# First unit in two sets of four, aggregation ahead of the last z2 store, and twelve last normalizations on VectorE in a GNN with LSTM windows

## The reference

```python
x = _layernorm(x + _L0_gnn_ref(...), axis=-1)      # x1
...
    agg = jnp.einsum('nm,bmd->bnd', A_hat, features)
    x = agg.reshape(-1, d)
    h = jax.nn.relu(_batchnorm(x @ W1.T + b1, g1, be1))
    out = h @ W2.T + b2
    out = _batchnorm(out, g2, be2)                 # over all graphs and nodes
...
x = _layernorm(x + _L1_gnn_ref(...), axis=-1)      # rows of 128 features
```

## Time and profile before

| | |
|---|---|
| median of 3 runs | 840.4 us (840.08 to 840.74) |
| the profiled execution's own time | 839.27 us |
| its span | 837.5 us |
| TensorE busy | 805.8 us, 96% |
| VectorE busy | 704.6 us, 84% |
| ScalarE busy | 593.3 us, 71% |
| GpSimd busy | 68.9 us, 8% |
| end of the last z2 store | 774.5 us |
| first scaling of the last stage | 777.2 us |
| last normalization ends | 835.0 us |

### The profile page before, as it was taken

How to read it: one execution, slowest core, us unless ns; L and a number is a source line. 1 busy time by engine, 2 the same in 40 slices (tenths; PEclk the granted TensorE clock), 3 DMA queues, 4 the chain that set the end, 5 groups by cost and what they waited for, 6 DMA issues and landing times.

```text
span 837.5 us, 15410 instructions
## 1 busy us (share of the span) xinstructions
PE 805.8 (96%) x4872; PEld 517.8 (62%) x4872; DVE 704.6 (84%) x1795; ACT 593.3 (71%) x1186; POOL 68.9 (8%) x58
## 2 busy tenths in 40 slices
PE   8999999999999999999999999999999977999984
PEld 7667677567757765776567657765675653333542
DVE  5678989888988898898889888998989986677995
ACT  4777777767776677767776777677776762990498
POOL 0000000000000000000000000000000001000674
PEclk9999999999999999999999999999999999999998
DMA  6000010201120012001100110011010110344244
GB/s 214 29 26 2 1 55 22 76 1 36 43 77 0 25 50 75 0 25 50 63 12 25 50 45 31 26 51 51 1 51 2 51 41 36 100 142 133 77 163 188
DMA packets 17691, 44.94 MB, mean 54 GB/s; under 512 B 2032, under 2 KB 3184, under 8 KB 17520
## 3 DMA queue, kind: packets, MB, share of 16 engines
q1 hardware_dynamic: 17648, 44.39, 14.9%
HBM read 27.61 MB, written 16.78 MB: 53 GB/s over the span
## 4 chain that ended last, share of the span: by engine, by line
PE 77%; issue 9%; DVE 9%; ACT 3%; SPq 1%; POOL 0%; DMA 0%; ACTq 0%; DVEq 0%; POOLq 0%
PE gate_bank L812 15%; PE gate_bank L813 15%; PE gate_bank L797 9%; PE gate_bank L828 6%; PE gate_bank L838 6%; PE back_bank L770 3%; PE front_bank L735 3%; PE front_bank L741 3%; PE front_bank L729 3%; PE front_bank L724 3%; DVE bn L1022 3%; PE gate_bank L821 3%; ACT z L940 2%; PE back_bank L778 1%; PE back_bank L780 1%
## 5 line engine op out<-in xcount | busy, mean ns | idle before, releaser
L812 PE MATMUL gate_bank<-h_hi,w_hi 128*128 128x256 f16 (+2 forms) x528 | 165.2, 313 | 5.1 <-DVE h_lo L1115 4.8
L813 PE MATMUL gate_bank<-h_hi,w_lo 128*128 128x256 f16 (+2 forms) x528 | 164.6, 312 | 0.0
L890 ACT ACTIVATE gate_i<-gate_bank,lstm_bias 128x256 f32<-128x256 f32 (+2 forms) x176 | 99.9, 572 | 71.1 <-PE gate_bank L838 58.7
L890 ACT ACTIVATE gate_o<-gate_bank,lstm_bias 128x512 f32<-128x512 f32 (+2 forms) x176 | 99.7, 571 | 35.5 <-PE gate_bank L838 21.1
L828 PE MATMUL gate_bank<-h_lo,w_hi 128*128 128x256 f16 (+2 forms) x384 | 117.7, 306 | 0.0
L1099 DVE SCALAR_TENSOR_TENSOR gate_f<-gate_o,gate_f 128x512 f32<-128x512 f32 (+2 forms) x176 | 95.1, 540 | 23.7 <-ACT gate_f L896 22.9
L812 PE MATMUL gate_bank<-s_hi,w_hi 128*128 128x256 f16 (+2 forms) x384 | 112.5, 301 | 0.5 <-DVE s_hi L1112 0.5
L813 PE MATMUL gate_bank<-s_hi,w_lo 128*128 128x256 f16 (+2 forms) x384 | 112.4, 301 | 0.0
L890 ACT ACTIVATE gate_g<-gate_bank,lstm_bias 128x256 f32<-128x256 f32 (+2 forms) x176 | 100.2, 569 | 6.3 <-PE gate_bank L838 3.3
L838 PE MATMUL gate_bank<-s_lo,w_hi 128*128 128x256 f16 (+2 forms) x384 | 102.4, 302 | 0.0
L896 ACT ACTIVATE gate_f<-cell 128x512 f32<-128x512 f32 (+2 forms) x176 | 88.8, 510 | 16.2 <-DVE cell L1090 9.8
(11 more groups left out here) (162 smaller groups left out, 1573.3 us busy)
## 6 DMA issues: line engine op xcount, KB each, us to landing
x_front<-in_x SPq DMA_DIRECT2D x16, 512.0 KB, 4.4
rows_sb<-in_x SPq DMA_DIRECT2D x16, 512.0 KB, 3.3
x_kept<-normed_sb SPq DMA_DIRECT2D x16, 512.0 KB, 2.7
z<-x_kept SPq DMA_DIRECT2D x16, 512.0 KB, 3.6
out<-z SPq DMA_DIRECT2D x15, 512.0 KB, 3.1
z<-in_wr SPq DMA_DIRECT2D x1, 1536.0 KB, 6.5
out<-z SPq DMA_DIRECT2D x2, 256.0 KB, 2.2
wih_sb<-in_wih SPq DMA_DIRECT2D x1, 192.0 KB, 2.4
```

The costliest lines, as they stand in the source:

```text
L812: mm(dst, w[0], v[0], start=start, stop=False)
L813: mm(dst, w[1], v[0], start=False, stop=False)
L890: ins = activation(acts[gate][h][:, 0:n], gate_bank[h][bank_of(job, gate)][:, 0:n], ACT.Tanh if gate == "g" else ACT.Sigmoid, bias=lstm_bi ...
```

## The change

Three edits in the stretch after the first part.

First, the z2 loop on VectorE runs one turn less and the last turn is written out. The last chunk's statistics signal by a semaphore of their own (`sem_bn2_all`), aggregation and the two small sums come right behind them, and the last chunk's store (`keep_z2`) stands behind the sums, ahead of the wait for GpSimd's power.

Second, the first unit is taken in two sets of four graphs (`first_terms`). VectorE makes two scalings (units 0 and 1), then statistics and moments of the first bank with the scaling of unit 2 behind step 1, then those of the second bank with the shift of the first four graphs behind step 0 and the scaling of unit 3 behind step 1, then the scaling of the first unit of pass 1. The shift of the other four stands in the next unit. GpSimd makes two powers of four columns for this unit, and ScalarE normalizes it in two parts. For this ScalarE's pass 0 is written out and its loop starts at 1. Semaphore counts of u = 0 are one signal (or four) higher from then on.

Third, in the last pass ScalarE normalizes units 0, 1 and four graphs of unit 2. VectorE normalizes the other four of unit 2 (`normed_here`, mean subtracted and rstd multiplied, so that no shift is needed) behind its last moments, then waits for the last power and normalizes the eight of unit 3. SyncE waits for `y_shared` and `y_norm[2]` before the store of unit 2; the last two stores wait for VectorE's `y_last`. The last shift is gone.

```diff
@@ semaphores, SyncE @@
+        sem_bn2_all = sem("bn2_moments_complete")
+        y_shared = sem("y_shared_normed")
...
-            for u in range(3):
+            for u in range(2):
                 store(HALVES // 4 - 1, u)
+            sp.wait_ge(y_shared, 1)
+            store(HALVES // 4 - 1, 2)
             for n in range(2):
                 sp.wait_ge(y_last, n + 1)
@@ GpSimd @@
             def row_powers(t, u):
-                pool.wait_ge(y_mom[u], 4 * t + 4)
+                if (t, u) == (0, 0):
+                    for n in range(2):
+                        at = slice(4 * n, 4 * n + 4)
+                        pool.wait_ge(y_mom[0], 4 * n + 4)
+                        nc.gpsimd.tensor_tensor(rstd[0][:, at], veps[0][:, at], neg_half[:, at], ALU.pow
+                                                ).then_inc(y_rstd[0], 1)
+                    return
+                pool.wait_ge(y_mom[u], 4 * t + 4 + 4 * (u == 0))
                 nc.gpsimd.tensor_tensor(rstd[u][:], veps[u][:], neg_half[:], ALU.pow).then_inc(y_rstd[u], 1)
@@ ScalarE @@
-            def normed_rows(t, u, last=False):
-                act.wait_ge(y_shift[u], t + 1)
-                for b in range(GB):
+            def normed_rows(t, u, graphs=range(GB)):
+                for b in graphs:
...
-                    if last and b == 3:
-                        ins.then_inc(y_last, 1)
-                ins.then_inc(y_last if last else y_norm[u], 1)
-
-            with act.Fori(0, HALVES // 4 - 1) as t:
+                return ins
+
+            def four_normed(t, first=False):
                 for u in range(4):
-                    normed_rows(t, u)
-            for u in range(4):
-                normed_rows(HALVES // 4 - 1, u, u == 3)
+                    if first and u == 0:
+                        for n in range(2):
+                            act.wait_ge(y_shift[0], n + 1)
+                            ins = normed_rows(0, 0, range(4 * n, 4 * n + 4))
+                    else:
+                        act.wait_ge(y_shift[u], t + 1 + (u == 0))
+                        ins = normed_rows(t, u)
+                    ins.then_inc(y_norm[u], 1)
+
+            four_normed(0, True)
+            with act.Fori(1, HALVES // 4 - 1) as t:
+                four_normed(t)
+            LAST = HALVES // 4 - 1
+            for u in range(2):
+                act.wait_ge(y_shift[u], LAST + 1 + (u == 0))
+                normed_rows(LAST, u).then_inc(y_norm[u], 1)
+            act.wait_ge(y_shift[2], LAST + 1)
+            normed_rows(LAST, 2, range(4)).then_inc(y_norm[2], 1)
@@ VectorE @@
+            with dve.Fori(0, CHUNKS // 2 - 1) as c:
                 for h in range(2):
...
+                    z2_stats(c, h)
+                    keep_z2(c, h)
+            z2_stats(CHUNKS // 2 - 1, 0)
+            keep_z2(CHUNKS // 2 - 1, 0)
+            z2_stats(CHUNKS // 2 - 1, 1).then_inc(sem_bn2_all, 1)
+            dve.wait_ge(sem_bn2_all, 1)
             ve.bn_aggr(mv[:, 0, :], z_moments[:, 0, :, :].rearrange("p c s -> p (c s)")).then_inc(sem_bn2, 1)
             dve.wait_ge(sem_bn2, 1)
             ve.tensor_tensor(small[:, 14:15], mv[:, 0, 0:1], v2_sb[:, 0:1], ALU.add)
             ve.tensor_scalar_add(small[:, 12:13], mv[:, 0, 1:2], EPS).then_inc(sem_bn2, 1)
+            keep_z2(CHUNKS // 2 - 1, 1)
             dve.wait_ge(sem_bn2_pow, 1)
...
+            def first_terms(n, between):
+
+                at = slice(4 * n, 4 * n + 4)
+                dve.wait_ge(y_full[0], n + 2)
+                row_stats(row_bank[0][n], bn[0], n).then_inc(y_mom[0], 1)
+                for step in range(3):
+                    dve.wait_ge(y_mom[0], 4 * n + step + 1)
+                    row_moments(bn[0][:, at, :], comb[0][:, :, at], veps[0][:, at], step).then_inc(y_mom[0], 1)
+                    between[step]()
...
+            def terms(t, u, scaled=True):
+                shift = (lambda: row_shift(t, u - 1) if u > 1 else row_shift(t + 1, 0)) if u else lambda: row_shift(t - 1, 3)
+                row_terms(t, u, (shift, (lambda: scale_z2(dve, 0, t + 1, u)) if scaled else nothing, nothing))
+
+            def normed_here(u, n):
+
+                for b in range(4 * n, 4 * n + 4):
+                    last = ve.tensor_scalar(z[:, CHUNKS - 8 + 2 * u + n, 1, (b % 4) * P:(b % 4 + 1) * P],
+                                            row_bank[u][n][:, (b % 4) * P:(b % 4 + 1) * P], comb[u][:, 2, b:b + 1],
+                                            rstd[u][:, b:b + 1], ALU.subtract, ALU.mult)
+                return last
+
+            dve.wait_ge(sem_bn2, 5)
+            for u in range(2):
+                scale_z2(dve, 0, 0, u)
+            first_terms(0, (nothing, lambda: scale_z2(dve, 0, 0, 2), nothing))
+            first_terms(1, (lambda: row_shift(0, 0, slice(0, 4)), lambda: scale_z2(dve, 0, 0, 3), nothing))
+            scale_z2(dve, 0, 1, 0)
+            row_terms(0, 1, (lambda: row_shift(1, 0, slice(4, 8)), lambda: scale_z2(dve, 0, 1, 1), nothing))
+            for u in range(2, 4):
+                terms(0, u)
+            LAST = HALVES // 4 - 1
+            with dve.Fori(1, LAST) as t:
                 for u in range(4):
-                    scale = nothing if last else lambda: scale_z2(dve, 0, t + 1, u)
...
+                    terms(t, u)
             for u in range(4):
-                scale_z2(dve, 0, 0, u)
-            LAST = HALVES // 4 - 1
-            four_rows(0, True, False)
-            with dve.Fori(1, LAST) as t:
-                four_rows(t, False, False)
-            four_rows(LAST, False, True)
-            row_shift(LAST, 3)
+                terms(LAST, u, False)
+            normed_here(2, 1).then_inc(y_shared, 1)
+            dve.wait_ge(y_rstd[3], LAST + 1)
+            for n in range(2):
+                normed_here(3, n).then_inc(y_last, 1)
```

More of the change, by code:

```diff
@@ L1037, in row_moments @@
                                                    op1=ALU.mult)
-                return ve.scalar_tensor_tensor(out=veps_t[:], in0=m2, scalar=1.0 / P, in1=apart, op0=ALU.mult,
+                return ve.scalar_tensor_tensor(out=veps_t, in0=m2, scalar=1.0 / P, in1=apart, op0=ALU.mult,
                                                op1=ALU.add)
@@ L1060, in back_rows @@
                     wait(dve, ("back", "moments", n - 1) if n else ("back", "stats", 1), g, h)
[L1061 removed]
+                    ins = row_moments(bn[0][:], comb[0][:], veps[0][:], n)
                 elif what == "normed":
@@ L1135, in _, with z2_stats, keep_z2 @@
             ve.tensor_tensor(small[:, 10:12], v1_sb[:, 2, :], small[:, 14:16], ALU.subtract).then_inc(sem_bn1, 1)
-            with dve.Fori(0, CHUNKS // 2) as c:
-                for h in range(2):
[L1140 to L1148, removed]
+            def z2_stats(c, h):
+                dve.wait_ge(z2_full[h], c + 1)
+                return ve.bn_stats(z_moments[:, 0, bass.ds(2 * c + h, 1), :].rearrange("p o s -> p (o s)"),
+                                   gate_bank[h][0][:])
+            def keep_z2(c, h):
+                ve.tensor_scalar(z[:, bass.ds(2 * c + h, 1), 0, :].rearrange("p o n -> p (o n)"),
+                                 gate_bank[h][0][:], v2_sb[:, 0:1], None, ALU.add).then_inc(z2_kept[h], 1)
+            with dve.Fori(0, CHUNKS // 2 - 1) as c:
+                for h in range(2):
+                    z2_stats(c, h)
[4 more added lines that the diff above has]
+            dve.wait_ge(sem_bn2_all, 1)
             ve.bn_aggr(mv[:, 0, :], z_moments[:, 0, :, :].rearrange("p c s -> p (c s)")).then_inc(sem_bn2, 1)
@@ L1177, in four_rows @@
-            def four_rows(t, first, last):
-                def nothing():
-                    pass
-                for u in range(4):
-                    scale = nothing if last else lambda: scale_z2(dve, 0, t + 1, u)
-                    if u:
-                        shift = lambda: row_shift(t, u - 1)
-                    else:
-                        shift = nothing if first else lambda: row_shift(t - 1, 3)
-                    row_terms(t, u, (shift, scale, nothing))
-            dve.wait_ge(sem_bn2, 5)
@@ new lines, in row_shift, with nothing @@
+            def row_shift(t, u, at=slice(0, GB)):
+                dve.wait_ge(y_rstd[u], t + 1)
+                ve.scalar_tensor_tensor(out=mean_rstd[u][:, at], in0=comb[u][:, 2, at], scalar=-1.0,
+                                        in1=rstd[u][:, at], op0=ALU.mult, op1=ALU.mult).then_inc(y_shift[u], 1)
+            def nothing():
+                pass
+            def terms(t, u, scaled=True):
+                shift = (lambda: row_shift(t, u - 1) if u > 1 else row_shift(t + 1, 0)) if u else lambda: row_shift(t - 1, 3)
+                row_terms(t, u, (shift, (lambda: scale_z2(dve, 0, t + 1, u)) if scaled else nothing, nothing))
```

7 lines of the change are left out of this document (2 added, 5 removed).

## The result

In seven runs each, the changed kernel has a median of 838.05 us (836.75 to 839.41), the kernel before 840.26 us (839.04 to 841.2). The ratio of the two is 0.9975 with a 95% interval of 0.9963 to 0.9987, so 2.1 us faster, between 1.1 and 3.1. A later set of runs of the same two kernels gave 838.71 against 839.71 us, 0.9990 (0.9978 to 1.0002), which alone could not tell the change from nothing. The forecast of 839.05 us said 1.35 us less.

A forecast was written before the change was run, and what follows sets the result against it. VectorE bounds the last stage until near 821 us, then ScalarE's backlog and the last stores. Tail -1.8 plus start offset +0.45 gives -1.35 us: from the median of 840.4 to 839.05 us, range 838.0 to 840.0.

The forecast's parts named there:

- Aggregation: VectorE after the last z2 statistics: aggregation ahead of the last z2 store starts 0.65 us earlier, the store covered.
- the second half: VectorE's second set of four in the first unit, with the first shift: 2.06 us.
- unit 1: VectorE's unit after the first, with the second shift: 2.86 us in place of 3.15, so -0.29.
- the hold by GpSimd: First unit: GpSimd's fourth scaling holds VectorE's small instructions up to 0.28 us; half taken, +0.14.
- the offset: VectorE's delay from the first units, carried through the steady part: +0.45 us, range 0 to +0.8.
- ScalarE's early start: ScalarE begins the first unit at about 782.5, not 784.9; worth nothing at the end.
- Tail: Last pass, twelve rows moved to VectorE: -1.8 us with the stores, -2.3 by arithmetic alone.
- Queue: Last stores at the kernel's end: their queue ends 0.5 us later than arithmetic alone.
- (b): Rival: the start keeps its gain (offset 0) or arithmetic binds the tail (-2.3): 838.4 us, chance 0.25.
- (a): The forecast: stores bind the tail and the start loses its gain: 839.05 us, 838.5 to 839.6, chance 0.56.
- (c): Rival in the tail: VectorE's normalization out of PSUM holds GpSimd's last power up to 1.2 us: 839.75, chance 0.12.
- (d): Rival: GpSimd's scaling falls on VectorE's in each steady unit, +5.3 us, total 844.4, chance 0.04.

The follow-up runs named there:

- the run with 12 fillers and the last reload apart: Changed kernel with 12 TensorE fillers, not 20, and the last x1 reload waited for ahead of the last pass alone: stretch 62.35 us, ratio 0.9976.
- the sets of four alone: Kernel before with only the first unit taken by sets of four: stretch 64.76 us, 0.45 longer than before, ratio 0.9998.
- the run without the store: Changed kernel without the 512 KB store of the third last-pass unit, that output left unwritten: stretch 62.23 us, against 62.70; no ratio.
- the run with both cut: Changed kernel with the second and third last-pass units' stores cut in 256 KB halves, VectorE's half of the third first: stretch 62.27 us, ratio 0.9968.
- the run with one cut: Changed kernel with the second last-pass unit's store cut in two of 256 KB: stretch 62.70 us, no change; no ratio.
- the last run above: Changed kernel, first unit whole, two stores cut, last eight graphs shared by VectorE and ScalarE, last reload awaited before last pass only: stretch 60.98 us, ratio 0.9964.

## Why the prediction was right, step by step

The direction and what binds came as forecast, the size a little better: forecast -1.35, stretch -1.61, time -2.1 (1.1 to 3.1). By the time alone the likeliest case did not come: 838.05 us lies below its own range of 838.5 to 839.6 and only 0.05 inside the whole range of 838.0 to 840.0, and the same kernel had 838.71 in the later set. That it fell inside is in part luck; the stretch and the separate runs carry the account.

**Aggregation.** Forecast 0.65 earlier; measured +0.73 in place of +1.46, so 0.73. The store is covered as said: VectorE's next instruction starts at 776.88, 0.03 behind the power. The step of the prediction that the gain is lost at TensorE is right, the reason was wrong. It said that the fillers end later (777.35) than the reload lands (about 777.0). With 12 fillers the transpose did not move; the reload lands later than its median from the DMA view says. The number survived by luck (forecast +4.36, measured +4.48), because the two ends lie close together: the fillers alone allow +4.11.

**Sets of four.** First statistics +6.01 forecast, +6.00 measured; first half 1.96 and 1.96; power of four columns 1.03 forecast, 1.01 measured. Three terms were too large: the second half (2.06, measured 782.16 to 784.13, 1.97), unit 1 (2.86, measured 784.58 to 787.36, 2.78), and the hold by GpSimd, +0.14, which did not occur. That last term rested on GpSimd's scalings keeping their 0.93 us. With no scaling of VectorE's beside them the third and fourth took 0.76, and were over at 780.98, before VectorE's small instructions at 781.13. The mechanism itself is real: it cost 0.23 in the run with 12 fillers and the last reload apart (0.40 in place of 0.17) and 0.21 in the sets of four alone (0.38), where the small instructions came before GpSimd was through. The rule of the exclusive lock in the Trainium skill ("SBUF — State Buffer", "Who interferes with whom") agrees with these two rows. Together the offset was +0.45 forecast and +0.12 measured. With it the forecast would have been -1.8 + 0.12 = -1.68 us against the stretch's -1.61: the offset was the term that was mis-sized. Counted from the fillers' start the offset is even nothing: the third unit begins 786.23 - 772.87 = 13.36 us behind it before, and 787.36 - 774.00 = 13.36 after. By that count TensorE's first transpose came just where it was forecast (4.68 behind, 777.55 in the times of before), and the end -1.73 against -1.8.

Two slips in the working did no harm. The bounds of the offset, 0 to +0.8, don't follow from their own terms: TensorE at 777.4 without a hold gives 0.31 - 0.15 = 0.16, TensorE at 777.87 with the full hold 0.31 + 0.32 + 0.28 = 0.91; the +0.12 lies below them. And 385 GB/s is not the highest rate in the slices of before, some have 393.

**What the sets of four cost.** The prediction's claim that ScalarE's early start is worth nothing is shown: leaving the sets out brings VectorE's third unit 0.72 earlier (+12.44 in place of +13.16) and makes the stretch 0.70 shorter, so nothing of the early start is left at the end. One at a time the parts give -0.66, -1.75 and +0.45, sum -1.96; together -1.61. Most of the missing 0.35 is the aggregation's gain, which needs the four scalings: with them it moves the first statistics from +7.13 to +6.42, by 0.71, and without them from +6.20 to +6.00 only. Of the 0.51 lost there 0.21 comes back, because the hold by GpSimd falls away. At the third unit it is 0.70 against 0.41 (+13.57 to +13.16). The last 0.06 is less than one kernel's stretch moves.

**Tail.** ScalarE's last four end at 824.83 + 7.12 = 831.95, +57.75; forecast +57.66 and the offset. VectorE's normalization out of PSUM has a pitch of 1.28 / 4 = 0.32, within the bounds of 0.257 and 0.349, taken at 0.30. Queue: 0.5 forecast, 0.43 to 0.47 measured, by the run without the store and the run with both cut. The prediction had the third unit's data follow the second's by 0.03 us; the run with one cut showed that it is the issue of the third unit's store that counts.

**The rivals.** (b), the start keeps its gain or arithmetic binds: arithmetic is out, the tail lost its 0.45. The start came between (a) and (b), at +0.12 by the stretch; counted from the fillers it is the 0 that (b) says. But not for (b)'s reason: TensorE started at 777.55 and not by 777.4, and it was the smaller terms above and the 0.12 of the written-out turn that made it up. So (a) is right on the tail and too pessimistic on the start. (c), VectorE holds GpSimd's last power: the power of 829.70 took 1.64 beside four normalizations out of PSUM; it is out, and the same section of the Trainium skill, which says that a VectorE instruction with at most one SBUF input, outside the two-port modes, does not contend, agrees. (d), a slower steady unit: from 787.36 to 790.54 are 3.18, as before; out.

What stays open is why the time ahead of the stretch scatters from 771.35 to 775.20 us between executions. The granted clock of TensorE differs with it. Two rows of 60 us, from the kernel before and from the last run above (the third column from the right is the granted clock):

```profile
660.00:720.00 60.00, 49.31 (x284) 28.37 (x282) 43.94 (x119) 33.33 (x64) 3.97 (x3) 0.94 0.11 40
```

```profile
660.00:720.00 60.00, 50.16 (x290) 27.94 (x289) 45.73 (x122) 33.68 (x65) 3.97 (x3) 0.97 0.12 44
```

In slices of 1 us the clock falls between 674 and 719 us to 0.50, the lower of its two levels (1.2 in place of 2.4 GHz): for 3.4 us in all in the two executions with the early start, for 6.8 in seven others, for 10.2 in the remaining five. Ahead of its one fall the last run had TensorE busy 5.82 of the 8 us from 685 to 693; so had the kernel before, where none followed. Single runs say the same: of the eleven with 12 fillers and the last reload apart, the three under 836 us had a mean granted clock of 0.995, the eight over 837 us 0.991 to 0.994. That goes with the two early starts, but not with the order of the others: those with 6.8 us begin the last statistics at 773.19 to 774.34, those with 10.2 at 773.40 to 775.20. Nothing was aimed at it, so it is read beside the time and not shown as its cause. It speaks against an effect of the edits, as do the medians of the two kernels with the reload apart (837.85 and 836.31 us), which lie 2.3 and 2.1 above their profiled executions.

## What to carry to other kernels

An edit that starts a downstream engine earlier is worth nothing if another engine sets its pace from there on; look at whether it idles before each steady unit, and at what the edit takes away from the engine that does set the pace. Work that stands ahead of a wait can be its cover: two scalings moved behind it turned into 1.35 us of idling. When an edit of 1 or 2 us sits at the end of a long kernel, measure from an event just ahead of it: here the time before that event moved by 2.0 us over twelve executions (3.9 with the two early ones), and the stretch behind it, in two executions of the same kernel, by 0.24. Check that the edit leaves the event itself where it is: counted from another engine's event, this one had moved by 0.12.

## What the runs showed of the hardware

- A 512 KB store that finds the queue empty has its first data 1.2 us after its issue began (issued 831.28, data from 832.5), a 256 KB store after 0.85 us (the last one of the run without a store: issued 833.78, data from 834.6). The issue itself takes SyncE 0.57 and 0.34 us of that. The data move at some 385 GB/s (full slices of 320 to 401); a store issued while another's data move shows no gap. Cutting the last large stores in halves gave 0.43 us.
- GpSimd's power takes 0.56 us for one column, 1.01 for four and 1.64 for eight, by estimate 0.15 a column over a fixed 0.4. The second power of four columns took 1.25 in the changed kernel: it started at 784.29, while a VectorE scaling of 784.13 was running.
- GpSimd's scaling of 512 columns takes 0.93 us beside VectorE's scalings and 0.76 while VectorE idles or takes statistics out of PSUM. Over two scalings that gave 0.34 us back to GpSimd, which was then through 0.15 before VectorE's small instructions.
- A VectorE instruction of 4 columns, begun while GpSimd's scaling ran, took 0.40 or 0.38 in place of 0.17 us and ended with it.
